# A fused AdaLN block: another order at the front's step borders, gates of three quarters in its last steps, the back's channel scaling on ScalarE

## What is computed

```python
h = layernorm(x) * (1 + ca) + sa                       # per sequence: ca, sa, ...
q, k, v = (silu(causal_conv(h @ W, taps)) for W in (Wq, Wk, Wv))
beta = sigmoid(h @ Wb)
delta = delta_rule_chunkwise(q, k, v, beta, chunk=32)   # 8 heads of 16 channels
short, long = fir(v, 3 taps), fir(v, 31 taps)
floor = sigmoid(h @ floor_W + floor_b) * 0.2
fus = gelu(h @ fus_W1 + fus_b1) @ fus_W2 + fus_b2       # 4 logits per head
p = sigmoid(fus[3]) * (1 - floor)
ctx = softmax(fus[0:3]) * (1 - p)
o = ctx[0]*short + ctx[1]*long + ctx[2]*delta + p*v
x = x + ga * (rms(rms(o)) @ Wo)
h = layernorm(x) * (1 + cb) + sb
x = x + gb * moe(h)                                     # router, top-k, 16 experts
```

## Time and profile before

| | us |
|---|---|
| median of 3 runs | 997.2 (994.96 to 997.96) |
| profiled execution, its own time | 1000.62 |
| span of its instructions | 998.6 |
| PE busy | 799.1 (80%) |
| DVE busy | 760.6 (76%) |
| ACT busy | 430.7 (43%) |
| POOL busy | 157.4 (16%) |

### The profile page before, as it was taken

How to read it: one execution, slowest core, us unless ns; L and a number is a source line. 1 busy time by engine, 2 the same in 40 slices (tenths; PEclk the granted TensorE clock), 3 DMA queues, 4 the chain that set the end, 5 groups by cost and what they waited for, 6 DMA issues and landing times. The chain is left out here.

```text
span 998.6 us, 43330 instructions
## 1 busy us (share of the span) xinstructions
PE 799.1 (80%) x19441; PEld 502.9 (50%) x19441; DVE 760.6 (76%) x1664; ACT 430.7 (43%) x840; POOL 157.4 (16%) x212
## 2 busy tenths in 40 slices
PE   3898899989989899999855465697987641999982
PEld 2344465555555555655555465554543300666782
DVE  6255999888999888999998835889898637677641
ACT  4577555455556564544421021366756621211100
POOL 2100101001001000000000000011111104777752
PEclk9999999999999999999987666699899765999996
DMA  4410101111110100101000003954545231344477
GB/s 117 74 33 23 34 25 41 43 38 39 37 52 30 40 26 30 42 30 42 25 31 5 22 18 100 287 134 109 136 108 142 59 93 26 101 116 124 66 177 182
DMA packets 96913, 71.25 MB, mean 71 GB/s; under 512 B 18216, under 2 KB 83416, under 8 KB 96728
## 3 DMA queue, kind: packets, MB, share of 16 engines
q1 hardware_dynamic: 88536, 61.40, 21.8%
q0 software_dynamic: 6080, 6.04, 3.6%
q10 hardware_dynamic: 2112, 1.05, 0.4%
HBM read 39.99 MB, written 28.46 MB: 69 GB/s over the span
## 5 line engine op out<-in xcount | busy, mean ns | idle before, releaser
L733 PE MATMUL ps_p<-hT,Wconv 128*128 128x512 f32 x384 | 192.2, 629 | 7.4 <-PEq L114 7.1
L841 DVE TENSOR_TENSOR f_L<-f_L,f_prod 128x60 f32<-128x60 f32 (+14 forms) x240 | 121.1, 505 | 8.3
L838 DVE TENSOR_TENSOR f_prod<-f_L 128x60 f32<-128x60 f32 (+14 forms) x240 | 118.9, 496 | 6.0
L733 PEld LDWEIGHTS ps_p<-hT,Wconv 128*128 128x128 f32 x384 | 69.9, 195 | 80.2 <-issue 74.8
L1417 POOL DMA_INDIRECT got<-xh_dram,slot_row x64 | 61.2, 956 | 52.8 <-DVEq L1556 33.6
L699 PE MATMUL ps_a<-f_TT,f_r 32*32 32x64 f32 x2048 | 40.4, 242 | 18.0 <-DVE f_r L869 11.1
L1501 ACT ACTIVATE act_g<-pe_g 128x512 f32<-128x512 f32 x32 | 17.4, 595 | 81.6 <-PE pe_g L1465 81.6
L699 PEld LDWEIGHTS ps_a<-f_TT,f_r 32*32 32x32 f32 x2048 | 37.1, 124 | 27.6 <-issue 16.0
L550 POOL TENSOR_SCALAR f_ln<-f_mv 128x4 f32<-128x4 f32 x12 | 4.1, 346 | 282.5 <-DVE f_mv L969 282.5
L1425 POOL DMA_INDIRECT out_dram<-y_slots,slot_row x28 | 44.7, 1598 | 20.9 <-DMA out_dram<-y_slots,slot_row 12.2
L1180 PE MATMUL b_ps_y<-b_v_rest,fir 32*32 32x64 f32 x768 | 42.1, 285 | 4.3 <-DMA b_v_rest<-v_tok_dram 4.3
(11 more groups left out here) (325 smaller groups left out, 1950.8 us busy)
## 6 DMA issues: line engine op xcount, KB each, us to landing
w<-in_L_ffn_w_dram SPq DMA_DIRECT2D x48, 128.0 KB, 2.5
s_tok_dram<-f_s_tok SPq DMA_DIRECT2D x16, 256.0 KB, 2.1
o_tok_dram<-f_o_tok SPq DMA_DIRECT2D x16, 256.0 KB, 2.3
b_s_in<-s_tok_dram SPq DMA_DIRECT2D x16, 256.0 KB, 2.9
b_o_in<-o_tok_dram SPq DMA_DIRECT2D x16, 256.0 KB, 3.0
b_x_in<-_attn_hidden_states_dram SPq DMA_DIRECT2D x64, 64.0 KB, 2.1
out_dram<-b_x SPq DMA_DIRECT2D x64, 64.0 KB, 1.8
xh_dram<-b_xh SPq DMA_DIRECT2D x64, 64.0 KB, 1.8
```

Of the source, the lines that this page charges most:

```text
L733: last = pe.matmul(ps[:, :], g.Wconv[:, which, tap, :], tokens(t, tap), start=(tap == 0), stop=(tap == TAPS - 1))
L838: dve.tensor_tensor(tmp, M[:, :, m + 1:, m:m + 1].broadcast_to([P, 2, rows, cols]), M[:, :, m:m + 1, 0:cols].broadcast_to([P, 2, rows, col ...
L841: dve.tensor_tensor(M[:, :, m + 1:, 0:cols], M[:, :, m + 1:, 0:cols], tmp, ALU.add).then_inc(s["solved"], 1)
```

## The change

1. Front, borders of steps: TensorE does k's first half before `sm`, and turns x between s and q's first half. The list of bank uses becomes k, sm, v, x, q, f0, f1, dense. VectorE turns `sm` after the short FIR. ScalarE writes `hT` after the state and ahead of q's silu.
2. Gates: the logits of quarters 1 and 2 are loaded back by SP in step 12 into the two `hT` buffers, unused by then; steps 14 and 15 do all of three quarters (a loop over `g.kept`), and the back makes only quarter 3's, in step 8.
3. Back: the scaling by channel becomes 16 activations of 32 columns each on ScalarE, between the copy of the router logits and the square.

```diff
-            for kind, n in [("sm", unit(i + 4))] + [(x, unit(i + 5)) for x in ("k", "v", "q", "f0", "f1")] + [("x", tile(i + 5)), ("dense", unit(i + 5))]:
+            for kind, n in [("k", unit(i + 5)), ("sm", unit(i + 4)), ("v", unit(i + 5)), ("x", tile(i + 5))] + [(x, unit(i + 5)) for x in ("q", "f0", "f1", "dense")]:
...
+                if i == NCH - 4:
+                    need(sp, s["dense_ps"], NCH - 1)
+                    for sem in sm_out:
+                        sp.wait_ge(sem, 16 * (NCH // 2 - 2))
+                    for j in (1, 2):
+                        sp.dma_start(g.kept[j].logits.rearrange("p (t n) -> p t n", t=4), a.logits[4 * j:4 * j + 4].rearrange("t p n -> p t n")).then_inc(logits_in[j - 1], 16)
...
                 if i == NCH - 2:
...
+                    for j, kept in enumerate(g.kept):
+                        if j > 0:
+                            act.wait_ge(logits_in[j - 1], 16)
+                        act.activation(kept.nq.rearrange("p (n g) -> p n g", g=G2), kept.logits.rearrange("p (n r) -> p n r", r=16)[:, :, 14:16],
+                                       ACT.Sqrt, bias=g.eps_l2[:, :]).then_inc(s["q_root"], 1)
+                    for j, kept in enumerate(g.kept):
+                        need(act, s["shifted"], j)
+                        act.activation(kept.gate[:, :, 3], kept.gate[:, :, 3], ACT.Tanh, scale=0.5)
+                        act.activation(kept.floor, kept.floor, ACT.Tanh, scale=0.5)
+                        act.activation(kept.gate[:, :, 0:3], kept.gate[:, :, 0:3], ACT.Exp).then_inc(s["gates_exp"], 1)
...
                 if i == NCH - 1:
...
+                    for j, kept in enumerate(g.kept):
+                        need(dve, s["q_root"], j)
+                        then(dve.reciprocal(kept.nq, kept.nq))
+                        need(dve, s["gates_exp"], j)
+                        then(weigh_gates(dve, then, kept.gate, kept.floor, kept.top, kept.nq))
...
+                if n is not None:
+                    need(act, s["t_ps"], n)
+                    need(act, s["r1_ps"], n - 2)
+                    for b in range(NB):
+                        last = act.activation(seqs(hT[n % 2])[:, b, :], seqs(ps_t)[:, b, :], ACT.Copy, scale=g.mod[:, CB, b:b + 1])
+                    last.then_inc(s["hT_ready"], 1)
...
-                if n is not None:
-                    need(dve, s["t_ps"], n)
-                    need(dve, s["r1_ps"], n - 2)
-                    dve.tensor_tensor(seqs(hT[n % 2]), seqs(ps_t), g.mod[:, CB, :].unsqueeze(2).broadcast_to([P, NB, C]), ALU.mult).then_inc(s["hT_ready"], 1)
...
-                    if t % 4 == 0 and t // 4 + 1 < 4:
-                        gates_before(t // 4 + 1)
+                    if t == 8:
+                        gates_before()
```

More of the change, by code:

```diff
@@ L441, in stage_front @@
         s_out, sm_out, o_out = ([nc.alloc_semaphore(name=f"f_{n}_out{u}") for u in range(2)] for n in ("s", "sm", "o"))
-        own = [*s.values(), *xs_in, *v_out, *s_out, *sm_out, *o_out]
+        logits_in = [nc.alloc_semaphore(name=f"f_logits_in{u}") for u in range(2)]
+        own = [*logits_in, *s.values(), *xs_in, *v_out, *s_out, *sm_out, *o_out]
         quad = lambda q: slice(32 * q, 32 * q + 32)
@@ L677, in _ @@
                     take_valid(o_tok[i % 2], o_wide).then_inc(s["o_copied"], 1)
-                if n is not None:
-                    need(act, s["x_ps"], n)
-                    need(act, s["dense_ps"], 4 * (n // 4) - 1)
-                    need(act, s["halo_ready"], n - 4)
-                    ps = ps_p[bank["x", n]]
-                    for m in range(4):
-                        b = 4 * (n % 4) + m
-                        last = act.activation(hT[(n // 4 + 1) % 2][:, b, TAPS - 1:], ps[:, m * P:(m + 1) * P], ACT.Identity,
-                                              bias=g.mod[:, SA, b:b + 1], scale=g.mod[:, CA, b:b + 1])
-                    last.then_inc(s["h_ready"], 1)
                 if t is not None:
@@ L784, in _ @@
                         .then_inc(s["s_ps"], 1)
+                if n is not None:
+                    ps = free_bank(pe, "x", n)
+                    need(pe, s["xh_ready"], n)
+                    for m in range(4):
+                        last = pe.transpose(ps[:, m * P:(m + 1) * P], xh[:, m, :], g.ident[:, :])
+                    last.then_inc(s["x_ps"], 1)
                 if i == -1:
@@ L807, in _ @@
                     long_fir(3)
-                if n is not None:
-                    ps = free_bank(pe, "x", n)
-                    need(pe, s["xh_ready"], n)
-                    for m in range(4):
-                        last = pe.transpose(ps[:, m * P:(m + 1) * P], xh[:, m, :], g.ident[:, :])
-                    last.then_inc(s["x_ps"], 1)
                 if t is not None:
@@ L893, in _ @@
                     dve.transpose(s_tok[t4 % 2][:, :], short[:, :]).then_inc(s["s_turned"], 1)
+                if t4 is not None:
+                    need(dve, s["sm_ps"], t4)
+                    need(dve, s["beta_ready"], t4 - 2)
+                    need(dve, s["inv_step"], 2 * (t4 - 2))
+                    need(dve, s["sm_halved"], t4 - 2)
+                    dve.transpose(sm_tok[t4 % 2][:, :, :].rearrange("p b r -> p (b r)"), ps_p[bank["sm", t4]][:, :]).then_inc(s["sm_turned"], 1)
                 if t3 is not None:
```

134 lines of the change are left out of this document (65 added, 69 removed).

## The result

| | before | after |
|---|---|---|
| median of the timed runs, us | 997.58 (4 runs) | 1011.73 (1007.46 to 1013.82, 4 runs) |
| ratio | | 1.0149, 95% interval 1.0107 to 1.0190 |
| profiled execution, us | 1000.62 | 1013.82 |
| its span, us | 998.6 | 1012.0 |

The account below looks back on a forecast made before the run. Front and back were each taken as near a balance of two engines, so waits count. Filling steps +5, middle -8, front's end +7.5 and back +3.2 sum to +7.7 on 997.2: 1005 us, range 988 to 1013.

Parts of the forecast that it names:

- Filling steps: Front's steps before the first full step: new bank dependences and later small rows make TensorE late, +5 us, bounds 0 and +7.
- Middle: Front's full steps: new border order removes 11.1 us of VectorE waits, about 3 come back; -8 us, bounds -14 and -3.
- tail: End of the front: two more weighings in step 15 before the last output turn; +7.5 us, bounds +6 and +9.
- Level: Rival: border order pays in full (-14), filling steps lose 2; 996 us; chance 0.17 with the last rival's better half.
- Front's end: Steps 14 and 15: extra shifting free, two more weighings (9.7 us) less 2.1 us idle; +7.5 us, bounds +6 and +9.
- Back's start: Back, first steps: quarter 1's gates gone, less load ahead of v, but TensorE is late there; -2 us, bounds 0 and -7.
- Rounds: Back, thirteen rounds from square to square: sixteen activations take 3.0 us, ScalarE bounds plain rounds at 10.4 us; sum +2.7 us.
- Drain: End of the back: hT stands twice in the chain, each 2.3 us longer, partly hidden; +2.5 us.
- ScalarE's idle covers the sixteen: Rival for the back: sixteen activations at 2.2 us, ScalarE's round 9.04; -10.5 us in all, 987 us; chance 0.18.
- It doesn't do what it says: Rival: the gates' move only shifts 14.6 us of VectorE work; 1000 us if the back's start gave its 7 us.
- ScalarE dear: Rival for the back: 0.30 us per activation, +27 us in place of +3.2; 1029 us; chance 0.07.

Follow-up runs that it names:

- after_fill: Changed kernel plus four extra 512-column TensorE products in the last filling step, where it waits for k's silu; 1008.21 us, ratio 1.0096.
- after_sm_first: Changed kernel, but VectorE turns the small rows ahead of the short FIR, as before; 1007.55 us, ratio 1.0103.
- gates_spread: gates with step 15's three weighings spread: before the turn of u, between it and the last output turn, and behind that; 991.63 us, ratio 0.9938.
- gates: Kernel before with part 2 alone: gates of three quarters in the front's last steps, borders and scaling as before; ratio 1.0001.
- scale_one: Kernel before, with ScalarE copying the turned rows in one 512-column activation, channel scaling left out; plain rounds 9.52 to 9.55 us.
- scale_24: Kernel before with part 3 alone plus eight more such activations per unit, 24 for 16; rounds 12.1 to 13.5 us in place of plain ones.
- spread_early: Kernel before with part 1 in full steps only and part 2, weighings in step 14 and around step 15's turn of u; 984.09 us, ratio 0.9845.

## Why the prediction was right, and where not

Forecast 1005 us, slower, measured 1011.7: sign and main places were right, the sum was 7.7 where it is 14, near the upper end of what was forecast. It is that near partly by luck: against the trace's +13.4 the filling steps, the middle and the tail were taken 3.0, 5.0 and 2.7 us too low, the back 6.6 too high, and 1.6 us lie in the experts, which the change leaves alone. Step by step, against the row of after:

- **Filling steps, +5, measured +8.0.** The chain was as told: small rows behind the short FIR, silu of k at 125.9 by the forecast and ending 125.73 in the trace, TensorE waiting for it. The step that failed is the end of that sum: what a wait costs TensorE behind it. The clock fell, 3 us (after_fill). The late turn of the small rows is 5.1 of the 8.0 us (after_sm_first), these 3 among them.
- **Middle, -8, measured -3.0 (-3.4 over fourteen executions).** Of the 11.1 us of VectorE's waits 10.5 went, as said. Of what comes late next I priced only the second score product, 3 us; 11.6 us came back (4.4 at the second score product, 4.1 at u, 3.1 at r). I missed that the freed TensorE runs into the turn of `L`: 13.2 us of waits there in place of 16.0 before `sm`. A list of TensorE's waits, with the question which release comes next, was missing. What gain is left goes with the clock, which the sum for the middle left out and only the rival *Level* named. And the late turn of `sm` that I made responsible for the loss costs nothing here (after_sm_first).
- **Front's end, +7.5, measured +8.1 to +8.9 in the runs with this tail, +10.2 in the changed kernel's own.** Mechanism and size right. The 1.7 us more in that one trace lie in the step from 530.8 to 557.7 (26.9 against 25.2); the same step took 26.2 in gates_spread and after_sm_first and 25.0 in the others, whatever part they held, so it is scatter.
- **Back's start, -2, measured -6.5 (-5.0 in gates alone).** Mis-sized: both stalls of TensorE shrank, 2.7 and 1.8 us, and I had credited half of that. It lay within the bounds. Part of it is only put off: the round just behind took 1.6 us more (12.96 against 11.37; 2.0 more in gates).
- **Rounds, +2.7, measured +0.4 over the thirteen that the forecast adds up** (the table's +2.0 has the round before them too). The plain round is 10.03 against a forecast of 10.4, since the sixteen take 2.80 us (0.169 each from start to start: 2.80 less one duration of 0.26, by 15) and not 3.0, and overlap their neighbours: ScalarE's busy time in the round rose by 2.49. Three others took 10.7 to 11.0 where 10.4 was expected.
- **Drain, +2.5, measured +1.1 here, +2.9 and +6.2 in two other pairs.** Its length depends on whether the clock falls in it.

The Trainium skill, "ScalarE: Activation LUTs", section "What ACT_TABLE_LOAD costs", by which each activation would be an estimated 0.213 us, comes out too high for this form: 0.169 measured, below my own 0.19 too.

**The rivals.** *ScalarE's idle covers the sixteen* needed a round of 9.04; scale_one shows that with VectorE relieved and ScalarE hardly loaded TensorE holds the plain round at 9.5. The row was there: 9.46 of 9.46 busy in the earlier trace rows. That VectorE held the round before was not wrong, but TensorE stood right behind it. With that the rival had no ground at all, and part 3 could only lose. *Level* asked the border order for -14 and got -3.4. *It doesn't do what it says*, that the gates' move is only a shift, had the right idea: the back's start gave 6.5 of its 7 us (4.9 with the round behind it), but against the tail's 8.5 the whole of part 2 is level, and what decides is the place of the weighings, which is worth 8 us. *ScalarE dear* was wrong in the price of one activation, 0.30 against 0.169; what dearer scaling would do, scale_24 showed with its rounds of 12.1 to 13.5 us.

## What to carry to other kernels

- Take a wait off one engine and it runs to the next buffer that somebody empties: list that engine's waits by line before and ask for each which release comes next. Here 16.0 us of TensorE's waits became 13.2 at the next bank, and the gain that was left went with the clock.
- Work that moves into a stage's last step is free only ahead of the last handover, in an idle stretch that is long enough; behind it, it delays the end of the stage, with the loads of the next. The same three weighings cost 8.5, 3.3 or 0.7 us by place.
- Relieving an engine pays only if another isn't at its limit already: TensorE without idle in a plain round was the sign that the scaling's move had nothing to gain.

## What the runs showed that was not expected

- In a wait of 1.94 us, behind 11.8 us of dense products, TensorE fell to 0.50 of its clock (1.2 instead of 2.4 GHz) for 6.8 us (the stretches above); with the wait filled by products that nobody needs, the first full step opened 2.7 us sooner.
- The back's plain round has two lengths with the same instructions. In gates_spread all ran at 9.47, all but one with a clock of 1.00; in spread_early four in a row took 10.24 at 0.83:

```profile
671.87:682.10 10.23, 10.23 (x180) 5.82 (x172) 8.63 (x22) 6.94 (x11) 1.26 (x2) 0.83 0.55 139
...
728.72:738.18 9.46, 9.46 (x173) 5.57 (x174) 8.42 (x22) 6.84 (x11) 1.26 (x2) 1.00 0.51 136
```

The first router product then takes 1.68 us (1.12 else) in each such round. What starts and ends such a row of rounds stays open. Such rounds are 3 to 4 us of the scatter between executions of one kernel, and the drain's two lengths (24.6 and 27.3 us) another 3.
